# The middle stage of a graph and attention layer: work moved one step further ahead, and the inverse root by logarithm and exponential

## The reference, cut to what matters

```python
xn = layernorm(x)                                    # x: 12500 x 256
x = x + gnn(xn, src, dst) + linear_attention(xn)     # gather two rows per node; 8 heads of elu + 1
h = layernorm(x)
logits = h @ gate_w + gate_b                         # 8 experts
probs = softmax(logits); idx = argmax(probs); prb = probs[idx]
pos = cumsum(one_hot(idx))[idx] - 1                  # place of a token in its expert's list
y = expert_mlp(buf[idx, pos]) * prb                  # two matmuls per expert, 256 -> 1024 -> 256
x = x + y
```

## Time and profile before

| | before |
|---|---|
| median of 3 runs | 1539.72 us (1539.47 to 1540.53) |
| the profiled execution | 1540.95 us, its span 1539.1 us |
| PE busy | 1426.4 us, 93% |
| DVE busy | 1122.5 us, 73% |
| ACT busy | 952.0 us, 62% |
| POOL busy | 727.3 us, 47% |
| granted TensorE clock, mean | 0.943 |

### The profile page before, as it was taken

How to read it: one execution, slowest core, us unless ns; L and a number is a source line. 1 busy time by engine, 2 the same in 40 slices (tenths; PEclk the granted TensorE clock), 3 DMA queues, 4 the chain that set the end, 5 groups by cost and what they waited for, 6 DMA issues and landing times. The chain is left out here.

```text
span 1539.1 us, 30428 instructions
## 1 busy us (share of the span) xinstructions
PE 1426.4 (93%) x9008; PEld 1282.6 (83%) x9008; DVE 1122.5 (73%) x2832; ACT 952.0 (62%) x2017; POOL 727.3 (47%) x704
## 2 busy tenths in 40 slices
PE   5999999998799898899579999999999999999995
PEld 4999999997677777777469999999999999999994
DVE  5888888883678778778536867767776776877764
ACT  2555555542477777777556767667676676767662
POOL 1100000003788888888243446445446445455533
PEclk8999999997788988988779999999999999999998
DMA  4434333333344444445312121213113131122000
GB/s 85 87 80 80 86 83 74 86 73 74 93 111 109 117 109 111 116 109 157 73 31 78 31 57 44 71 39 97 43 40 91 40 95 43 39 69 53 7 15 19
DMA packets 128116, 112.13 MB, mean 73 GB/s; under 512 B 66078, under 2 KB 113887, under 8 KB 127946
## 3 DMA queue, kind: packets, MB, share of 16 engines
q1 hardware_dynamic: 75206, 72.73, 19.0%
q0 software_dynamic: 52864, 38.82, 11.5%
HBM read 76.17 MB, written 43.85 MB: 78 GB/s over the span
## 5 line engine op out<-in xcount | busy, mean ns | idle before, releaser
L1390 POOL DMA_INDIRECT out<-q_all,to_i x128 | 176.3, 1378 | 328.6 <-issue 293.8
L1592 DVE TENSOR_TENSOR h_lo<-q_all,h_hi 128x496 fp32r<-128x496 f32 x256 | 173.8, 679 | 197.7 <-PE psY L1653 88.4
L1468 ACT ACTIVATE h_hi<-psH,b_sb 128x496 fp32r<-128x496 f32 x256 | 172.6, 674 | 232.7 <-PE psH L1676 225.7
L1653 PE MATMUL psY<-w_hi,h_hi 128*124 128x256 f32 x1024 | 289.2, 282 | 0.0
L1653 PE MATMUL psY<-w_hi,h_lo 128*124 128x256 f32 x1024 | 287.1, 280 | 0.0
L1653 PE MATMUL psY<-w_lo,h_hi 128*124 128x256 f32 x1024 | 286.8, 280 | 0.0
L1653 PEld LDWEIGHTS psY<-w_lo,h_hi 128*124 128x124 f32 x1024 | 188.9, 184 | 8.9
L1653 PEld LDWEIGHTS psY<-w_hi,h_hi 128*124 128x124 f32 x1024 | 188.8, 184 | 8.0
L1377 POOL DMA_INDIRECT q_all<-out,from_i x112 | 164.5, 1469 | 54.8 <-issue 54.8
L1653 PEld LDWEIGHTS psY<-w_hi,h_lo 128*124 128x124 f32 x1024 | 189.1, 185 | 0.0
L1470 ACT ACTIVATE q_all<-psH,b_sb 128x496 f32<-128x496 f32 x256 | 170.8, 667 | 0.0
(11 more groups left out here) (241 smaller groups left out, 3366.6 us busy)
## 6 DMA issues: line engine op xcount, KB each, us to landing
x_sb<-in_x SPq DMA_DIRECT2D x50, 448.0 KB
q_all<-in_L_ffn_w SPq DMA_DIRECT2D x16, 1024.0 KB
graph_table<-tab_sb SPq DMA_DIRECT2D x25, 511.0 KB
out<-xd SPq DMA_DIRECT2D x25, 448.0 KB
x_sb<-in_x SPq DMA_DIRECT2D x50, 52.0 KB
out<-q_all,to_i POOLq DMA_INDIRECT x128, 4.3
q_all<-out,from_i POOLq DMA_INDIRECT x112, 4.5
gl<-alpha_l_table,idx POOLq DMA_INDIRECT x100
```

Of the source, the lines that this page charges most:

```text
L1390: pool.indirect_dma_start(out=out, in_=o_sb[:, par, j, :], in_offset=None, out_offset=bass.IndirectOffsetOnAxis(ap=to_i[:, par, j:j + 1], ...
L1468: act.activation(h_hi[:, f % 4, :], psH[f % 2][:, 0:TS3], ACT.Relu, bias=b1_sb[:, bass.ds(e * NF + f, 1)]).then_inc(s_hhi_ready, 1)
L1592: nc.vector.tensor_tensor(h_lo[:, f % 4, :], hf[:, f % 4, :], h_hi[:, f % 4, :].bitcast(F32), ALU.subtract).then_inc(s_hlo_ready, 1)
L1653: ins = nc.tensor.matmul(psY[par][j // 2][0:T3, (j % 2) * D:(j % 2 + 1) * D], hh[:, f % 4, j * T3:(j + 1) * T3], w[:, f, :], start=f == 0 ...
```

## The change

- Inverse root: ACT takes Ln of variance plus eps and then Exp of minus one half of it, in place of Sqrt; DVE adds one Newton step (four small operations) in place of a reciprocal. One function set, which holds Ln and Exp, is loaded by name at the start of the stage.
- Further ahead: `q_copy` runs four tiles ahead, `q_ksum` three, `inverse`, `inverse_t`, `den_of` and `den_spread` two. `over_steps` writes the last five steps out.
- Order on DVE: `q_scaled(s+1)` comes ahead of `logits(s)`; in `place` the block is made before the sum and the reciprocal of the softmax.
- Order on PE: `q_ksum` comes between the third and the fourth part of `listed`; `den_spread(s+2)` follows `mix(s+1)`; `mix` loops over the contraction outside and the four groups inside, so it can begin with one half of `qp`.
- ACT: the last of four groups of one-hots is done after the root of the next tile; the copy of the gate's part of x moves here from POOL.
- POOL keeps only the gathers: token numbers come from tables made once, and the indices are brought by SP with one small DMA per tile.

```diff
             def over_steps(eng, step):
-                with eng.Fori(1, (NS - 3) // 2) as i:
-                    step(2 * i, 0, i, 2)
+                with eng.Fori(1, (NS - 5) // 2) as i:
+                    step(2 * i, 0, i, 4)
...
+                def idx_of(s, par, n):
+                    sp.wait_ge(gat[par], 32 * J * n)
+                    sp.dma_start(idx[:, par, :, :], idx_all[:, bass.ds(s, 1), :, :].rearrange("p a n j -> p (a n) j"))\
+                      .then_inc(idx_in[par], 16)
+                for s in range(2):
+                    sp.dma_start(idx[:, s, :, :], idx_all[:, s, :, :]).then_inc(idx_in[s], 16)
...
-                def token_of(s):
-                    pool.wait_ge(s_at_ready, 3 * J * s)
-                    nc.gpsimd.tensor_scalar(tokn[:, :], tokn[:, :], float(TS), None, ALU.add).then_inc(s_token, 1)
-                    nc.gpsimd.tensor_scalar(ntokn[:, :], ntokn[:, :], float(TS), None, ALU.subtract).then_inc(s_token, 1)
                 def step(s, par, h, ahead):
+                    if ahead > 1:
                         pool.wait_ge(s_pr, NPR * s + 1)
+                        gather(s + 2, par, h + 2)
-                        idx_of(s + 3, 1 - par, h + par + 1)
-                        xl_of(s + 2, par)
-                    token_of(s)
...
             def _(act):
+                act.preload_act_table_set("natural_log_exp_and_others")
...
                 def root(s):
-                    act.activation(std[:, :], mv[:, :, 1], ACT.Sqrt, bias=eps2[:, :]).then_inc(s_std2, 1)
+                    act.activation(std[:, :], mv[:, :, 1], ACT.Ln, bias=eps2[:, :]).then_inc(s_ln, 1)
+                    act.wait_ge(s_ln, s + 1)
+                    act.activation(std[:, :], std[:, :], ACT.Exp, scale=-0.5).then_inc(s_std2, 1)
...
                 def step(s, par, h, ahead):
                     root(s)
+                    hots(s - 1, J - 1)
+                    inverse_t(s + 2)
                     logit_exp(s)
                     att_exp(s + 1)
+                    q_copy(s + 4)
+                    xl_of(s + 2, par)
                     one_hots(s)
...
                 def logits(s):
                     dve.wait_ge(s_std2, s + 1)
-                    nc.vector.reciprocal(rstd[:, :], std[:, :]).then_inc(s_rstd2, 1)
+                    nc.vector.tensor_tensor(near[:, :], std[:, :], std[:, :], ALU.mult).then_inc(s_rstd2, 1)
+                    nc.vector.scalar_tensor_tensor(near[:, :], mv[:, :, 1], EPS, near[:, :], ALU.add, ALU.mult)\
+                    nc.vector.tensor_scalar(near[:, :], near[:, :], -0.5, 1.5, ALU.mult, ALU.add).then_inc(s_rstd2, 1)
+                    nc.vector.tensor_tensor(rstd[:, :], near[:, :], std[:, :], ALU.mult).then_inc(s_rstd2, 1)
...
                 def step(s, par, h, ahead):
                     rows_of(s, par, h)
+                        den_of(s + 2)
-                        den_of(s + 1)
+                        q_scaled(s + 1)
                     logits(s)
                     choose(s)
                         att_scores(s + 1, 1 - par, h + par + 1)
-                        q_scaled(s + 1)
                     place(s)
                         att_sum(s + 1, 1 - par)
...
                 def step(s, par, h, ahead):
                         x_part(s + 1, 1 - par, h + par + 1)
-                        inverse(s + 1)
-                        listed(s - 1, False)
-                        den_spread(s + 1)
+                        listed(s - 1, range(J - 1), False)
+                        q_ksum(s + 3, s + 2)
+                        inverse(s + 2)
+                        listed(s - 1, range(J - 1, J), False)
                     positions(s, ahead)
                         mix(s + 1)
-                        q_ksum(s + 2)
+                        den_spread(s + 2)
```

More of the change, by code:

```diff
@@ L659, in gps_layer @@
             rstd = sb2("rstdb", [T, J])
+            near = sb2("near", [T, J])
             lg = sb2("lg", [T, J, E])
@@ L773, in step @@
                     split_dma(sp, tok(out, s, D), xd[:, par, :, :], T, x_out[par])
-                    if ahead == 2:
+                    if ahead > 1:
                         sp.wait_ge(s_mix_mm, 2 * (s + 1))
                         load(s + 2, par)
-                    if ahead == 2 and isinstance(s, int) and s == NS - 3:
+                        if not (isinstance(s, int) and s + 3 >= NS):
+                            idx_of(s + 3, 1 - par, h + par + 1)
+                    if ahead > 1 and isinstance(s, int) and s == NS - 3:
                         first_expert()
@@ L821, in step @@
                 def step(s, par, h, ahead):
-                    if ahead == 2:
+                    if ahead > 1:
                         pool.wait_ge(s_pr, NPR * s + 1)
-                        gather(s + 2, par)
-                        if not (isinstance(s, int) and s + 3 >= NS):
-                            idx_of(s + 3, 1 - par, h + par + 1)
-                        xl_of(s + 2, par)
-                    token_of(s)
+                        gather(s + 2, par, h + 2)
                 over_steps(pool, step)
@@ L854, in _, with xl_of @@
                     act.activation(mix_w[:, c, :], psM[:, KC + c, 0:MW], ACT.Copy).then_inc(s_mixw_set, 1)
+                def xl_of(s, par):
+                    act.wait_ge(s_mix_mm, 2 * (s - 1))
+                    act.activation(x_sb[0:T, par, :, D:MW],
+                                   xl_all[:, bass.ds(s, 1), :, :].rearrange("p a j e -> p (a j) e"), ACT.Copy)\
+                       .then_inc(s_xl, 1)
                 def att_exp(s):
@@ L883, in one_hots @@
                     act.wait_ge(s_away, NAWAY * (s + 1))
-                    act.wait_ge(s_token, 2 * (s + 1))
                     passed(act, s_act_passed)
[L886 to L891, removed]
+                    for j in range(J - 1):
+                        hots(s, j)
                 def last_rows(s):
@@ L906, in step @@
                     root(s)
-                    if ahead > 0:
-                        inverse_t(s + 1)
+                    if not (isinstance(s, int) and s == 0):
+                        hots(s - 1, J - 1)
                     if ahead > 1:
-                        q_copy(s + 2)
+                        inverse_t(s + 2)
                     logit_exp(s)
@@ L1078, in _ @@
                 dve.wait_ge(s_bg_done, 2)
+                den_of(1)
                 att_scores(0, 0, 1)
@@ L1105, in _, with q_ksum @@
                     ins.then_inc(s_gt_mm, 1)
-                def q_ksum(s):
+                def q_ksum(s, copied):
                     pe.wait_ge(s_den_max, s)
-                    pe.wait_ge(s_inv_t, s)
+                    pe.wait_ge(s_inv_t, copied)
                     pe.wait_ge(s_q_cur, s + 1)
-                    if not (isinstance(s, int) and s < 2):
-                        pe.wait_ge(s_route, NROUTE * (s - 2) + 9)
+                    if not (isinstance(s, int) and s < 4):
+                        pe.wait_ge(s_route, NROUTE * (s - 4) + 8)
                     n = 0
@@ L1127, in _ @@
                 pe.wait_ge(s_dve_setup, 2)
-                q_ksum(0)
+                q_ksum(0, 0)
                 pe.wait_ge(s_gt_sb_done, KC)
@@ L1193, in positions, with listed @@
                     ins.then_inc(s_pos_mm, 1)
-                def listed(s, last):
-                    pe.wait_ge(s_at_ready, 3 * J * (s + 1))
-                    for j in range(J):
+                def listed(s, blocks, last):
+                    for j in blocks:
+                        pe.wait_ge(s_at_ready, 3 * J * s + (3 * (j + 1) if j < J - 1 and not last else 3 * J))
                         ins = nc.tensor.matmul(psP[0:T3, 0:2 * NB], at_row[:, j, :],
@@ L1221, in _ @@
                 pe.wait_ge(s_ctx_done, KC)
-                q_ksum(1)
+                q_ksum(1, 1)
                 x_part(0, 0, 1)
                 mix(0)
+                inverse(1)
+                q_ksum(2, 2)
+                den_spread(1)
                 pe.wait_ge(s_bg_done, 2)
                 over_steps(pe, step)
-                listed(NS - 1, True)
+                listed(NS - 1, range(J), True)
         with ExitStack() as ph, nc.Block() as block:
```

114 lines of the change are left out of this document (63 added, 51 removed).

## The result

The changed kernel takes 1523.87 us (median of 4 runs, 1521.91 to 1525.51) against 1540.12 us (1539.47 to 1540.58), ratio 0.9894, 95% interval 0.9877 to 0.9911: 16.3 us faster. The forecast was 19.6 us and 1520. The profiled execution took 1524.12 us, its span 1522.3.

The account below looks back on a forecast made before the run. The prediction took a loop of ACT and DVE to bound the middle stage at 14.42 us a step. 24 x (14.43 - 13.5) = 22.3, less 2.5 (start) and 0.2 (Newton), gave 19.6 us saved: 1520, range 1506 to 1534.

Parts of the forecast that it names:

- The bound before: Middle stage: ACT and DVE wait for each other in a loop, 8.93 plus 5.49 us, 14.42 us a step.
- The loop after: Middle stage: the ACT and DVE loop falls from 14.42 to about 10.9 us and is no longer the bound.
- The step: One tile of the middle stage: from 14.43 to a mean of 13.5 us, saving 22.3 us over 24 steps.
- max(13.0, 11.7 + loss): A step is the longer of DVE's work, 13.0 us, and PE's, 11.7 us plus mix's half clock loss, mean 1.5.
- the sum: Whole kernel: 22.3 us from the steps, less 2.5 at the start and 0.2 in the last tile, 19.6 us saved.
- Positions: DVE's place waits for PE's positions with less cover: between 0 and 0.3 us a step, nothing taken.
- The start: Middle stage's start: the first gather waits for an index DMA, at 370 to 372 us; 2.5 us lost, between 1 and 4.6.
- The marker: DVE's addition into xd, once a tile, used to time steps; it should come every 13.5 us.
- The end: Last tile of the middle stage: no load is waited for, but Newton is, costing 0.2 us.
- Full clock: Rival, middle stage: PE's clock comes back when its waits go; saving 31.6 us, 1508, chance 0.25.
- Half clock that spreads: Rival, PE in the middle stage: half clock runs from mix into den_spread; up to 1587, mostly near 1550, chance 0.08.
- 24 x 0.5 - 2.7: Rival, middle stage: more half clock, losses of 2.2 us a step; saving put at 9.6 us, 1530, chance 0.11.

Follow-up runs that it names:

- sqrt_back: The changed kernel with the old inverse root (Sqrt with two table loads a tile, one reciprocal, no Newton step): 1524.67 us.
- no_newton: The changed kernel without the Newton step, the Exp's result used as it is: 1521.96 us.
- start_order: The changed kernel with ACT taking att_exp(0) ahead of inverse_t(1) and q_copy(3) at the start of the middle stage: 1518.83 us.
- early_weights: start_order with the first expert's weights loaded in three parts behind tiles 20, 21 and 22, not at once behind tile 22: 1514.65 us.
- half_mix: The changed kernel with only the first half of the contraction in mix: 1534.11 us.
- ksum_first: all_three with q_ksum ahead of listed on PE, same instructions: median 1523.26 us, in two patterns 20 us apart.
- half_ksum: all_three with half of q_ksum's contraction left out: 1503.04 us.
- all_three: early_weights with the first two copies of the gate's part of x on ACT instead of behind sixteen gathers on POOL: 1508.35 us.

## Why the prediction was right, point by point

- **The bound before.** The loop of ACT and DVE was read rightly: shortening it by the token wait alone gave 11.7 us, by the root alone 3.0 us, both together 14.3 us, most of the whole 16.3.
- **The loop after.** As forecast it is no bound any more: ACT loads one set, at 367.20 us, waits for POOL never, and DVE waits for the root once, 0.6 us. ScalarE's two activations in the changed kernel:

```profile
572.84 0.30 ACT L868 ACTIVATE std<-mvb,eps 125x4 f32<-125x4 f32 x1 [1.01 <-DVE mvb L1015]
573.17 0.20 ACT L870 ACTIVATE std<-std 125x4 f32<-125x4 f32 x1
```

  They take 0.53 us from start to end, under the cover of `den_of` and `q_scaled`, which begins at 572.64. That the loads would be worth nothing once they are off the loop is shown by sqrt_back. The Trainium skill ("ScalarE: Activation LUTs", section "What ACT_TABLE_LOAD costs") puts a drain beside each load. The trace of before doesn't show one: the root starts 0.01 us after its load ends.
- **The step.** max(13.0, 11.7 + loss) gave 13.5 us; 13.29 was measured, with steps mostly of 12.8 to 13.0 and of 13.47 us, as the formula has them (13.0 and 13.4). The mean is lower since the losses were: mostly 0 or 1.7 us, and 2.9 us once, 1.0 in the mean where 1.5 was taken, with the clock of the stage at 0.89 to 0.91 rather than 0.87. Over 23 steps that is 25.3 us gained where 23 x 0.93 = 21.4 was in the sum.
- **Positions.** I took nothing for them, between 0 and 0.3 us. They cost 7.0 us in 18 tiles, 0.29 us a step, and are DVE's largest steady wait; I had named `mix`. Where they cost more, 22.2 us in sqrt_back and 20.9 in no_newton, a shorter list on DVE brings little or nothing.
- **The start.** The term of 2.5 us was the wrong one. The index DMA delayed the first gather to 370.27 us, as forecast (370 to 372), and `x_part(0)` by 1.1 us only. What cost more was the order on ACT, for which the sum has no term: I had counted ACT's spare time, without asking what each moved instruction waits for. The marker lost 9.15 us, of which start_order gives back 3 to 5 in the time.
- **The end.** 0.2 us was forecast for Newton; the wait for the last gather, present before with 1.7 us and now 4.5 us, wasn't in the sum. early_weights gives back 4.2 us.
- **The rivals.** Full clock: no, 0.91 from 410 to 720 us and 0.94 in the best stretch of 70 us, though steps with a fast `mix` came at DVE's pace as that case has it. Half clock that spreads: it didn't happen in this kernel, but half_mix and the slower pattern of ksum_first show that it was a real danger, by another way than I had named: not from `mix` into `den_spread`, but into `x_part` to `positions`.
- **Slips in the sums.** Three operations 0.23 us apart are 0.69 us, not 0.66; and 24 x 0.5 - 2.7 is 9.3, not 9.6. Neither moves a time by more than 1 us.

The saving came out 3.3 us under the forecast because the start was mis-sized by more than the steps were. In the two traces the steps gave 3.9 us more than was in the sum and the start took 6.7 us more. These misses have opposite signs, so that the number came so near is in part luck; the mechanism, a loop that goes and two lists that take over, is not.

## What to carry to other kernels

When work is moved further ahead, read each engine's list at its start and its end with the wait of every instruction: an instruction that is harmless in the steady step can wait there for something that comes only after the first tile, and all behind it wait too. When two lists are nearly as long as each other, a saving on one of them is given back in the next wait; test it by taking the work out before writing it. And the place at which an engine is slow counts as much as how long it is: look for the chain in which a block has no slack. Last, when the total moves, ask the marker where: in half_ksum the total fell as the theory said and the steps, which the theory was about, hadn't moved.

## What the runs showed of the hardware

- With half of its largest block taken out, TensorE's granted clock fell from 0.91 to 0.84 (410 to 720 us), and the kernel was 10 us slower than with the block.
- Two orders of the same instructions on TensorE ran at 0.91 and 0.85 over 430 to 700 us (all_three and ksum_first, one trace each), and the second had two times 20 us apart from run to run; the 0.85 is of its slower one.
- A table load took 1.28 us, and in the changed kernel the two functions of the set loaded by name followed each other without a load in all 25 tiles, in and out of the loop; the kernel before had 50 loads in the same stage.
